# A state-space scan over 64 steps: delta and dt x loaded four-fold from HBM, the decayed state kept in PSUM, and PE summing four steps at a time

## What is computed

```python
def step(h, inp):
    x_t, d_t, B_t, C_t = inp
    dA = jnp.exp(d_t[:, :, None] * A)
    h = dA * h + (d_t * x_t)[:, :, None] * B_t[:, None, :]
    y = jnp.einsum('bdn,bn->bd', h, C_t)
    return (h, y)
...
xs = jax.nn.silu(xs)
delta = jax.nn.softplus(dp @ Wdt + bdt)
A = -jnp.exp(A_log.astype(jnp.float32))
hidden = _ssm_scan(xs, A, Bs, Cs, delta)
y = (hidden + xs * Dp) * jax.nn.silu(z)
out = y @ Wout + bout
```

## Time and profile before

| | before |
|---|---|
| median of three runs | 2681.67 us |
| the profiled execution | 2681.49 us, span 2679.4 us |
| PE, DVE, ACT, POOL busy in the span | 89%, 62%, 40%, 36% |
| projections of the block | from about 1630 to 1765 us |
| scan | from 1774 to 2152 us |
| granted TensorE clock, mean of the span | 0.892 |

### The profile page before, as it was taken

The page is one execution under the profiler, slowest core; times in us unless marked ns, Lnnn a source line. Parts: engine busy times, 40 slices in busy tenths (PEclk is TensorE's granted clock), DMA queues, the critical chain, the costliest instruction groups (busy, mean ns, idle before and its releaser), DMA issues. The chain is left out here.

```text
span 2679.4 us, 65695 instructions
## 1 busy us (share of the span) xinstructions
PE 2379.7 (89%) x28672; PEld 1891.3 (71%) x28672; DVE 1659.6 (62%) x2685; ACT 1066.0 (40%) x1559; POOL 960.4 (36%) x660
## 2 busy tenths in 40 slices
PE   4999999999999999999999979679999974777773
PEld 2788888888888888888888854334444464677773
DVE  3555655555555555565555431858989846888885
ACT  1344444444444444444444424544444411222221
POOL 1122222212121212222121120359889712666661
PEclk9899999999999999999999989675656586988897
DMA  2011111111111111111111030043222114444443
GB/s 79 26 49 35 47 37 37 47 35 49 29 55 29 49 35 47 36 41 43 34 50 29 19 92 0 16 139 91 57 56 60 42 52 167 152 140 147 153 157 110
DMA packets 128313, 171.97 MB, mean 64 GB/s; under 512 B 17409, under 2 KB 108545, under 8 KB 127890
## 3 DMA queue, kind: packets, MB, share of 16 engines
q1 hardware_dynamic: 118242, 151.41, 19.0%
q0 software_dynamic: 4416, 12.06, 1.4%
q10 hardware_dynamic: 5392, 4.59, 0.6%
HBM read 128.05 MB, written 23.20 MB: 56 GB/s over the span
## 5 line engine op out<-in xcount | busy, mean ns | idle before, releaser
L453 POOL TENSOR_TENSOR ctx_lo<-ctx_whole,ctx_hi 128x768 fp32r<-128x768 f32 (+1 forms) x128 | 231.4, 1808 | 1120.9 <-DVE ctx_hi L476 1120.9
L493 DVE TENSOR_REDUCE max_part<-work 128x1 f32<-128x384 f32 (+1 forms) x1024 | 531.6, 568 | 80.2 <-PE work L619 62.9
L555 ACT ACTIVATE probs<-scores 128x1024 f32<-128x1024 f32 (+1 forms) x416 | 424.7, 1027 | 123.1 <-PE scores L644 123.1
L488 DVE SCALAR_TENSOR_TENSOR keys_lo<-work,bk,keys_hi 128x384 fp32r<-128x384 f32 (+1 forms) x256 | 162.5, 635 | 446.1 <-ACT keys_hi L535 446.1
L1150 POOL TENSOR_TENSOR xn_T<-delta_rep,xn 128x1024 f32<-128x1024 f32 x128 | 299.4, 2361 | 79.5 <-ACT xn L1167 36.9
L535 ACT ACTIVATE keys_hi<-work,bk 128x384 fp32r<-128x384 f32 (+1 forms) x256 | 152.5, 596 | 376.2 <-PE work L599 376.2
L638 PE MATMUL scores<-q_hi,keys_hi 64*128 64x256 f32 (+1 forms) x1664 | 273.5, 291 | 0.0
L658 PE MATMUL acc<-probs,values 128*17 128x64 f32 x13312 | 266.7, 221 | 7.1 <-ACT probs L555 7.1
L619 PE MATMUL work<-keys_hi,q_hi 64*128 64x384 f32 (+1 forms) x1024 | 256.5, 405 | 13.9 <-POOL q_lo L444 6.6
L638 PE MATMUL scores<-q_lo,keys_hi 64*128 64x256 f32 (+1 forms) x1664 | 262.3, 277 | 0.0
L638 PE MATMUL scores<-q_hi,keys_lo 64*128 64x256 f32 (+1 forms) x1664 | 262.2, 277 | 0.0
(11 more groups left out here) (231 smaller groups left out, 5191.0 us busy)
## 6 DMA issues: line engine op xcount, KB each, us to landing
xs<-in_w_T SPq DMA_DIRECT2D x46, 1024.0 KB, 6.5
ctx_whole<-in_ctx_T SPq DMA_DIRECT2D x96, 384.0 KB, 3.3
delta_rep<-delta SPq DMA_DIRECT2D x256, 64.0 KB, 2.0
ctx_whole<-in_ctx_T SPq DMA_DIRECT2D x32, 449.0 KB, 3.4
scratch_mixed<-mixed ACTq DMA_DIRECT2D x32, 128.0 KB, 1.8
mixed_b<-scratch_mixed SPq DMA_DIRECT2D x4, 1024.0 KB, 13.2
scratch_z<-z SPq DMA_DIRECT2D x16, 256.0 KB, 2.4
zg<-scratch_z SPq DMA_DIRECT2D x16, 256.0 KB, 3.0
```

Of the source, the lines that this page charges most:

```text
L453: nc.gpsimd.tensor_tensor(ctx_lo[c][:, :, 0:n], s.ctx_whole[c % 2][:, :, 0:n], ctx_hi[c][:, :, 0:n].bitcast(F32), ALU.subtract).then_inc(l ...
L488: nc.vector.scalar_tensor_tensor(keys_lo[par][:, m, start:start + n], bank[:, 0:n], s.bk[:, m:m + 1], keys_hi[par][:, m, start:start + n]. ...
L493: nc.vector.reduce_max(max_part[par][:, place(pair), c:c + 1], bank[:, 0:CHUNKS[c][1]], AX) \
L555: nc.scalar.activation(probs[slot][0:rows, :], scores[slot][0:rows, :], ACT.Exp, scale=1.0 / HD ** 0.5).then_inc(exp_done, 1)
```

## The change

Delta and dt x no longer stay in SBUF. `ssm_projections` stores each tile of both in HBM (32 stores of 256 KB, issued by SP ahead of the z stores), in a scratch tensor that the experts use later. `ssm_scan` loads them by pairs of steps, each step as one transfer whose source names the 32 rows four times (`to_broadcast`), into three buffers of two steps each, for delta and for dt x. PE's spread matmul is gone. DVE's product is written over the exponent in PSUM (`da`), and the multiply-add reads dt x from SBUF and the product from PSUM; the exponent of a half therefore waits for that half's multiply-adds of the step before. There are seven state buffers and eight of `c_diag`, and PE sums the states of four steps after the fourth (`sum_states`), 16 matmuls into one bank, which ACT copies once; PE then turns them with the identity (`turn`). The gate for a tile comes three steps later than before. SP loads z after an odd pair, behind the transfers of that pair.

```diff
@@ ssm_projections, SP
+            for n in range(TT):
+                for kept, made, out in ((s.delta, dt_done, of_steps(d, 0)), (s.dtx, dtx_done, of_steps(d, 1))):
+                    sp.wait_ge(made, n + 1)
+                    sp.dma_start(out[n * P:(n + 1) * P, :], kept[:, n, :]).then_inc(steps_stored, 16)
             for n in range(PIECES):
...
+            sp.wait_ge(steps_stored, 16 * 2 * TT)
@@ new
+def of_steps(d, i):
+    return d.results[2 * TOK * i:2 * TOK * (i + 1), :].rearrange("(r a) n -> r (a n)", a=2)
@@ ssm_scan
-        REP, CS = 4, 4
+        TWO, LOADS, CS, HS = 2, 3, 8, 7
@@ SP
-            for t in range(STEPS):
-                rows = slice(BATCH * (t % TILE_STEPS), BATCH * (t % TILE_STEPS + 1))
-                if t >= REP:
-                    sp.wait_ge(arg_done, 2 * (t - REP) + 2)
-                for q in range(NQ):
-                    sp.dma_start(delta_rep[t % REP][BATCH * q:BATCH * (q + 1), :], s.delta[rows, t // TILE_STEPS, :]) \
-                        .then_inc(delta_loaded[t % REP], 16)
-                if t == TILE_STEPS:
+            def load_steps(dst, i, pair, loaded):
+                rows = of_steps(d, i)[pair * TWO * BATCH:(pair + 1) * TWO * BATCH, :]
+                for t in range(TWO):
+                    sp.dma_start(dst[pair % LOADS][:, t, :],
+                                 rows[t * BATCH:(t + 1) * BATCH, :].rearrange("(a b) n -> a b n", a=1)
+                                 .to_broadcast([NQ, BATCH, INNER])).then_inc(loaded[pair % LOADS], 16)
+            for pair in range(STEPS // TWO):
+                if pair >= LOADS:
+                    sp.wait_ge(arg_done, 2 * TWO * (pair - LOADS + 1))
+                load_steps(delta_rep, 0, pair, delta_loaded)
...
+                if pair >= LOADS:
+                    sp.wait_ge(h_done, NG * TWO * (pair - LOADS + 1))
+                load_steps(dtx_rep, 1, pair, dtx_loaded)
+                if pair == 3:
                     sp.dma_start(s.wout[:, :, :], d.Wout.rearrange("(k p) n -> p k n", p=P)).then_inc(wout_loaded, 16)
...
-                if t == 4 * TILE_STEPS:
+                if pair == 9:
                     sp.wait_ge(x_stored, 16)
...
-                if t % TILE_STEPS == 0:
-                    load_z(t // TILE_STEPS)
+                if pair % 2 == 1:
+                    load_z(pair // 2)
@@ ACT
                     if t > 0:
-                        act.wait_ge(kept_done, 2 * (t - 1) + i + 1)
+                        act.wait_ge(h_done, NG * (t - 1) + 2 * (i + 1))
...
-                if t >= 2:
-                    copy_parts(t - 2)
+                if t >= 6 and t % TILE_STEPS == 2:
+                    copy_steps(t // TILE_STEPS - 1)
@@ DVE
-                    nc.vector.tensor_tensor(kept[i][:, :, :], da[i][:, :, :], before[:, 2 * i:2 * i + 2, :], ALU.mult) \
+                    nc.vector.tensor_tensor(da[i][:, :, :], da[i][:, :, :], before[:, 2 * i:2 * i + 2, :], ALU.mult) \
                         .then_inc(kept_done, 1)
-                dve.wait_ge(dtx_spread, t + 1)
-                if t >= 2:
-                    dve.wait_ge(parts_done, t - 1)
+                dve.wait_ge(dtx_loaded[pair % LOADS], 16 * (TWO * (pair // LOADS) + TWO))
+                if t >= HS:
+                    dve.wait_ge(steps_summed, (t - HS) // TILE_STEPS + 1)
...
-                if t >= 2 * TILE_STEPS - 2 and t % TILE_STEPS == TILE_STEPS - 2:
-                    gate(t // TILE_STEPS - 1)
+                if t >= 2 * TILE_STEPS + 1 and t % TILE_STEPS == 1:
+                    gate(t // TILE_STEPS - 2)
+            gate(TT - 2)
             gate(TT - 1)
@@ PE
+            def sum_states(n):
+                pe.wait_ge(c_diag_done, TILE_STEPS * (n + 1))
+                if n >= 2:
+                    pe.wait_ge(steps_copied, n - 1)
+                pe.wait_ge(h_done, NG * TILE_STEPS * (n + 1))
                 for g in range(NG):
+                    for i in range(TILE_STEPS):
+                        t = n * TILE_STEPS + i
+                        last = nc.tensor.matmul(y_steps[n % 2][BATCH * i:BATCH * (i + 1), :], c_diag[t % CS][:, g, :],
+                                                h[t % HS][:, g, :], start=(g == 0), stop=(g == NG - 1),
+                                                skip_group_check=True)
+                last.then_inc(steps_summed, 1)
...
+            for n in range(TT):
+                sum_states(n)
+                turn(n)
```

More of the change, by code:

```diff
@@ L1076, in sem @@
             return ctx.enter_context(nc.semaphore(name))
-        REP, CS = 4, 4
+        TWO, LOADS, CS, HS = 2, 3, 8, 7
         b_of, c_of = sb("b_of", [P, NG, STEPS]), sb("c_of", [P, NG, STEPS])
-        same_batch, spread = sb("same_batch", [P, BATCH]), sb("spread_batch", [P, NQ, BATCH])
+        same_batch = sb("same_batch", [P, BATCH])
         skip = sb("skip", [P, KI, P])
-        delta_rep = [sb(f"delta_rep{i}", [P, INNER]) for i in range(REP)]
+        a_wide = sb("a_wide", [P, NG, INNER])
@@ L1083, in ssm_scan @@
+        delta_rep = [sb(f"delta_rep{i}", [P, TWO, INNER]) for i in range(LOADS)]
+        dtx_rep = [sb(f"dtx_rep{i}", [P, TWO, INNER]) for i in range(LOADS)]
         c_diag = [sb(f"c_diag{i}", [P, NG, BATCH]) for i in range(CS)]
-        kept = [sb(f"kept{i}", [P, 2, INNER]) for i in range(2)]
-        part = [sb(f"y_part{i}", [P, INNER]) for i in range(2)]
+        arg = [sb(f"arg{i}", [P, 2, INNER]) for i in range(2)]
+        part = [sb(f"y_tokens{i}", [P, INNER]) for i in range(2)]
         z = [sb(f"zg{i}", [P, KI, P]) for i in range(2)]
-        a_rep, h, arg = s.a_rep, s.h, s.arg
+        a_rep = s.a_rep
@@ L1212, in _ @@
             for t in range(STEPS):
-                before, after = h[(t + 1) % 2], h[t % 2]
+                pair = t // TWO
+                before, after = h[(t - 1) % HS], h[t % HS]
                 for i in range(2):
@@ L1247, in sum_quarters @@
-            def sum_quarters(t):
-                pe.wait_ge(h_done, NG * (t + 1))
-                pe.wait_ge(c_diag_done, t + 1)
-                if t > 0:
-                    pe.wait_ge(parts_copied, t)
-                for g in range(NG):
-                    last = nc.tensor.matmul(y_parts[BATCH * g:BATCH * (g + 1), :], c_diag[t % CS][:, g, :],
-                                            h[t % 2][:, g, :], start=True, stop=True, skip_group_check=True)
-                last.then_inc(parts_done, 1)
@@ L1257, in sum_up @@
-            def sum_up(t):
-                n, step = divmod(t, TILE_STEPS)
-                if step == 0:
-                    if n >= 2:
-                        pe.wait_ge(y_done, n - 1)
-                    for k in range(KI):
-                        nc.tensor.matmul(y[n % 2][:, k, :], skip[:, k, :], s.xs[:, k, n * P:(n + 1) * P],
-                                         start=(k == 0), stop=False, skip_group_check=True)
-                pe.wait_ge(parts_copied, t + 1)
-                for k in range(KI):
-                    last = nc.tensor.matmul(y[n % 2][:, k, step * BATCH:(step + 1) * BATCH],
-                                            part[t % 2][:, k * P:(k + 1) * P], same_batch[:, :],
+            def sum_states(n):
+                pe.wait_ge(c_diag_done, TILE_STEPS * (n + 1))
+                if n >= 2:
+                    pe.wait_ge(steps_copied, n - 1)
+                pe.wait_ge(h_done, NG * TILE_STEPS * (n + 1))
+                for g in range(NG):
+                    for i in range(TILE_STEPS):
[4 more added lines that the diff above has]
+                last.then_inc(steps_summed, 1)
@@ new lines, in turn @@
+            def turn(n):
+                if n >= 2:
+                    pe.wait_ge(y_done, n - 1)
+                for k in range(KI):
+                    nc.tensor.matmul(y[n % 2][:, k, :], skip[:, k, :], s.xs[:, k, n * P:(n + 1) * P],
+                                     start=(k == 0), stop=False, skip_group_check=True)
+                pe.wait_ge(steps_copied, n + 1)
+                for k in range(KI):
+                    last = nc.tensor.matmul(y[n % 2][:, k, :], part[n % 2][:, k * P:(k + 1) * P], s.ident[:, :],
```

100 lines of the change are left out of this document (41 added, 59 removed).

## The result

The changed kernel takes 2709.43 us, the median of four runs (2709.32 to 2710.70), beside 2681.48 for the kernel before (2675.76 to 2684.14, four runs). The ratio is 1.0108, 95% interval 1.0091 to 1.0126: slower by 1.1%, where 2715 was forecast. The profiled execution took 2709.32 us, with a span of 2707.6; against the span before, 2679.4, it is 28.2 us longer.

A forecast was written before the change was run, and what follows sets the result against it. It took PE's chain at the low clock, plus SP's wait on the gate, to bound the kernel. 2681.5 + 26.5 (loop) + 5.7 (scan end) + 1 (after) + 0.5 (projections) = 2715.2, say 2715 us; range 2646 to 2740.

The forecast's parts named there:

- Four engines: Delta and dt x loads with four copies outermost run on four DMA engines; chance 0.66, 2696 to 2740 us.
- A round of 24.2: Scan, four steps from gate to gate with late delta: 24.2 us, against 20.8 free and about 23.1 before.
- The bump before step 8: Scan: wout, bout and the x store delay pair 4's delta to 1825.4, where POOL wants it at 1814.3.
- The x loads: Scan, four x loads at pair 9: 10.3 us of engine time, putting about 9 us on one round.
- E of step 63: End of the scan's last multiply-add: forecast at 2174.4, 26.5 us later than 2147.86.
- The in-place wait: Scan: second exponent waits for its half's multiply-adds, adding 0.21 us to 4.89, so 5.10 us a step.
- the 20.8 of the prediction: Scan: length in us of a round of four steps when no delta is late.
- That rival: Scan product in PSUM: reading and writing one bank takes two turns, 137 us more, 2788 us; chance 0.03.
- The end of the scan: Last multiply-add to last gate's end: sixteen sums start late, 10 us instead of 4.35, +5.7 (2.6 to 8.3).
- After the scan and in the projections: Next matmuls may start at the low clock, +1 us (0 to 3); stores may delay z, +0.5 (0 to 3).
- The rival with sixteen engines: Scan's 256 KB loads spread over all engines, no round late: 2651 us (2646 to 2657); chance 0.20.
- what bounds the kernel before: Scan before: PE's low-clock chain and SP standing on DVE's gate cost 0.9 us a step over DVE's pace.

The follow-up runs named there:

- two copies: Changed kernel with each load of a step cut in two, each with two copies of the 32 rows (128 KB): 3024.13 us, a single run.
- other rows: Changed kernel, but a transfer's four blocks of 32 rows are four different blocks, in the same shape: 2711.37 us.
- the gate's wait gone: Changed kernel with three buffers for z instead of two, transfers still on four engines: 2695.46 us, ratio to before 1.0062.
- the free kernel: Changed kernel with loads by quarter (outermost dimension 32, sixteen engines) and three z buffers: 2639.62 us, ratio to before 0.9850.
- the run with sixteen engines: Changed kernel with one transfer for each quarter with both steps (source [32, 2, 512]), same bytes: 2646.13 us, ratio to before 0.9869.

## Why the prediction was right, point by point

- **Four engines (shown).** The step on which all hung. Share and rate say four at 24.4 to 24.8 GB/s (24.0 was taken), half as many for two copies, the same for other rows, and another shape with the same bytes takes 63 us off. No row of the kernel before could decide it, and the prediction gave it 0.66. The rule of the Trainium skill that the prediction weighed (DMA: Bandwidth & Descriptors, the table of rules near its end) agrees; it speaks of any outermost dimension under 16, with the broadcast as an example, and the run with other rows shows that too.
- **A round of 24.2 (right).** Measured 23.4 to 24.2, on average 23.8. Its make-up holds: landing 8.8 us behind the gate where 8.5 was taken, then 15.2 where 15.45 was; with the gate's wait gone most rounds are 22.1 to 22.5, the engines' own time. Only the 0.3 us for the second pair of a round does not appear: POOL waits 0.5 us for it, and DVE goes through without a gap.
- **The bump before step 8 (right).** The gate after step 9 was to end at 1840.9; it ended at 1840.34, with the scan 1.6 us earlier. The prediction's landing of 1825.4 is 0.8 more than its own terms give (1766.3 + 58.3 = 1824.6).
- **The x loads (undersized).** The round was to take 33.2 us and took 36.9. By the rows of SP's issues the step left out SP: its four issues held it for 12.46 us and the z behind them for 5.20, so the next delta was issued at 1895.96 only. The ten ordinary rounds behind it, 0.4 us shorter than forecast on average, pay these 3.7 us back, and that is luck.
- **E of step 63 (right, helped by luck):** 2174.4 forecast, 2173.55 measured. Two errors of 3.7 us cancel in it, and 1.6 us come from the earlier start, so that from step 0 on the loop grew by 27.3 where 26.5 was forecast.
- **The in-place wait (a size off).** A free step takes 5.01, not 5.10: the second exponent comes 0.12 us late for DVE, not 0.21. The gate round of the free kernel, 20.52, lies 0.3 under the 20.8 of the prediction. PSUM read and written by one operation costs next to nothing: the product takes 1229 ns on average, against 1215 into SBUF before. That rival is out.
- **The end of the scan.** +4.9 where +5.7 was forecast; 9.2 us were measured, 10 taken between 12.6 and 6.9. The granted clock of this stretch is 0.70, between the two levels as taken.
- **After the scan and in the projections.** +1 and +0.5 were forecast. The stores of delta and dt x cost nothing: the last z was made at 1759.78, 1.6 us earlier like all that went before. Behind the scan it was 2.4 us less, not more: here the prediction had the sign wrong. It expected the first matmuls behind the scan at a lower clock than before, and they had a higher one. The 8 us behind the last gate, before and after:

```profile
2152.00:2160.00 8.00, 7.47 (x25) 6.25 (x26) 1.05 (x3) 1.28 (x1) 7.49 (x11) 0.69 0.03 3
2182.80:2190.80 8.00, 7.70 (x36) 6.82 (x37) 1.68 (x4) 1.28 (x1) 7.71 (x12) 1.00 0.03 3
```

The clock is 0.69 and 1.00, and DVE's first operation of the next stage starts 4.18 us after the gate before and 2.40 after. That is 1.8 of the 2.4 us; the rest is open. The spans grew by 28.2 us where 33.7 were forecast: 1.6 of these 5.5 us are the earlier start, 3.4 the stages behind the scan, 0.5 the projections, while the loop and its end miss by 0.8 each, in opposite directions.

- **The rival with sixteen engines.** Worked out at 2651 (2646 to 2657); the kernel built to that rule took 2646.1. So the gain that the change aims at is there, 36 us in the loop (327.7 against 364.0). The shape of the delta and dt x loads turned it into a loss of 27.
- **Where the prediction was wrong: what bounds the kernel before.** It put SP's wait for the gate beside PE's chain. The trace showed POOL's 33.7 us of waits for delta, but they were all covered: POOL has 0.8 us a step to spare at the mean pace of 5.78, and the run with three z buffers left the loop at 364.0. The forecast was not hurt, since its sum was made on absolute times.

## What to carry to other kernels

Before a transfer replaces an engine's work, look at its outermost dimension: here loads with four in it ran on four DMA engines and loads with two on the same two, whatever the number of transfers, while those with 32 and 128 in it used all. The DMA share times sixteen, held against the rate, suggests how many engines carry a stage, and a run that changes only the shape settles it; a share of a quarter is no free capacity if it is four full engines. And a wait in the list of waits is a cost only if its waiter has no slack until the next hand-over: take one cause away and look whether the time moves.

## What the runs showed of the hardware that was not expected

- DVE and GpSimd take turns at SBUF when DVE reads two tensors from it: 0.74 us became 1.82 beside GpSimd's products, 264 us for this kernel. The parts of the change are tied by this. Beside POOL's products dt x in SBUF pays only with the product in PSUM, and the old kernel, with dt x in PSUM and the product in SBUF, also had one input in each. The in-place part was not tried alone in the kernel before: both inputs of its multiply-add would lie in PSUM, a form that no kernel here has.
- Issues hold SP while the few engines are full: an issue of a 256 KB load took 0.5 us right after a gate and 2.5 to 2.8 behind the first four, and one of the 512 KB x loads 3.1. With two copies an issue of 128 KB took 2.2 to 2.9 us, and with the loads on sixteen engines four issues of 128 KB took mostly 1.7 to 1.9 us in all. That SP waits there for room in the queues is a reading; no run shows it.
- An engine moves 24.4 to 24.6 GB/s of 2 KB rows when it is full, with two engines at work as with four, and a kernel that reads different blocks of rows instead of one for all copies keeps the same pace (2711.4 us against 2709.4). With all sixteen busy it moves less: 14.6 GB/s of 2 KB rows (234 in all, in the run with sixteen engines). What limits it there was not tried.
